# Order of two steps on TensorE in the attention loop of a four-layer graph network: the scores of two steps in a row, then the value products and denominators of two steps

## The reference

```python
q = (x @ Wq + bq).reshape(n, H, DK)          # H = 8 heads, DK = 64
k = (x @ Wk + bk).reshape(n, H, DK)
v = (x @ Wv + bv).reshape(n, H, DK)
logits = einsum('ehd,ehd->eh', q[rows] / sqrt(DK), k[cols]) + att_bias
p = exp(logits - row_max[rows])
denom = segment_sum(p, rows)
y = segment_sum((p / denom[rows])[:, :, None] * v[cols], rows)
out = y.reshape(n, 512) @ Wo + bo
```

## Time and profile before

| | |
|---|---|
| median of three runs | 1270.24 us |
| the three runs | 1258.51, 1270.24, 1271.98 us |
| span of the profiled execution | 1264.5 us |
| time of the profiled execution outside the span | none is given |
| TensorE busy | 1203.6 us (95%) |
| VectorE busy | 864.5 us (68%) |
| ScalarE busy | 431.7 us (34%) |
| stretch from the first scores of the loop to the end | 282 us, from 982.6 us on |

### The profile page before, as it was taken

The page is one execution under the profiler, slowest core; times in us unless marked ns, Lnnn a source line. Parts: engine busy times, 40 slices in busy tenths (PEclk is TensorE's granted clock), DMA queues, the critical chain, the costliest instruction groups (busy, mean ns, idle before and its releaser), DMA issues.

```text
span 1264.5 us, 22058 instructions
## 1 busy us (share of the span) xinstructions
PE 1203.6 (95%) x8483; PEld 547.2 (43%) x8484; DVE 864.5 (68%) x1180; ACT 431.7 (34%) x585; POOL 309.5 (24%) x220
## 2 busy tenths in 40 slices
PE   6989888999898999999999999999999999999997
PEld 2334333323443343344445454454332455555563
DVE  7577666434444555552478874658999799899897
ACT  1445556322232221213301003145551454444344
POOL 2001110000010243454555654555462000000000
PEclk9989999999998999999999999999999899999999
DMA  8568885798798788643122213113222666465552
GB/s 325 208 225 301 292 298 165 281 358 310 244 360 284 276 313 278 220 97 114 3 50 35 50 3 69 2 2 44 33 33 56 234 206 230 167 203 198 189 181 107
DMA packets 64414, 222.78 MB, mean 176 GB/s; under 512 B 31226, under 2 KB 36090, under 8 KB 48360
## 3 DMA queue, kind: packets, MB, share of 16 engines
q1 hardware_dynamic: 34794, 156.40, 35.6%
q0 software_dynamic: 25184, 53.10, 16.5%
q10 hardware_dynamic: 4350, 12.07, 2.8%
HBM read 198.94 MB, written 59.94 MB: 205 GB/s over the span
## 4 chain that ended last, share of the span: by engine, by line
PE 64%; DVE 11%; DMA 10%; issue 8%; SPq 5%; ACT 3%; ACTq 0%; DVEq 0%
PE PS L1812 24%; PE PS L1761 10%; PE PS L2057 4%; PE PS L1616 4%; PE PS L2044 4%; DMA R<-R 4%; DVE R L1147 4%; DVE R L1182 3%; PE PS L1634 3%; SPq L602 3%; PE PS L1686 2%; PE PS L1926 2%; SPq L600 2%; PE PS L2077 2%; PE PS L2106 2%
## 5 line engine op out<-in xcount | busy, mean ns | idle before, releaser
L787 POOL DMA_INDIRECT bias_d<-R x160 | 272.9, 1706 | 331.5 <-DMA bias_d<-R 220.2
L1812 PE MATMUL PS<-R 128*128 128x512 f16 x1300 | 298.4, 381 | 0.0
L1812 PEld LDWEIGHTS PS<-R 128*128 128x128 f16 x1300 | 120.5, 98 | 180.5 <-issue 49.8
L1572 ACT ACTIVATE R<-PS 128x1024 f32<-128x1024 f32 (+1 forms) x100 | 100.4, 1005 | 144.0 <-PE PS L2044 143.9
L1686 PE MATMUL PS<-R,XX 125*128 125x512 f16 (+2 forms) x612 | 131.0, 344 | 16.2 <-ACT R L1361 7.5
L1761 PE MATMUL PS<-W,XX 128*128 128x512 f16 x600 | 136.1, 386 | 4.7 <-DVE R L985 2.7
L1182 DVE SCALAR_TENSOR_TENSOR R<-R,W 128x1024 f32<-128x1024 f32 (+1 forms) x68 | 133.9, 1985 | 8.7 <-ACT R L1572 7.2
L1147 DVE CUSTOM_DVE_ANT_0 R<-PS,R 128x1250 f16<-128x1250 f32 x80 | 116.8, 1460 | 5.5 <-PE PS L1980 2.9
L901 DVE TENSOR_SCALAR R<-W,R 125x1250 f16<-125x1250 f16 x160 | 89.5, 606 | 42.4 <-PE PS L1686 27.6
L2044 PE MATMUL PS<-R 128*128 128x256 f16 (+3 forms) x800 | 107.4, 277 | 1.4 <-DVE R L1147 1.1
L2057 PE MATMUL PS<-R 128*32 128x256 f32 (+1 forms) x1600 | 105.7, 382 | 0.7 <-DVE R L1182 0.3
(11 more groups left out here) (226 smaller groups left out, 1395.6 us busy)
## 6 DMA issues: line engine op xcount, KB each, us to landing
bias_d<-bias_d POOLq DMA_DIRECT2D x39, 1280.0 KB, 8.5
R<-in_basis_s SPq DMA_DIRECT2D x32, 1024.0 KB, 6.6
W<-in_basis_s SPq DMA_DIRECT2D x28, 1024.0 KB, 6.3
W<-bias_d SPq DMA_DIRECT2D x27, 1024.0 KB, 4.9
R<-bias_d SPq DMA_DIRECT2D x13, 1024.0 KB, 5.0
R<-key_d SPq DMA_DIRECT2D x20, 500.0 KB, 3.8
R<-R SPq DMA_DIRECT2D x120, 80.0 KB, 5.9
W<-bias_d SPq DMA_DIRECT2D x7, 904.0 KB, 4.6
```

The source lines that it names most:

```text
L787: pool.indirect_dma_start(bias_d, bass.IndirectOffsetOnAxis(ap=idx[:, c:c + 1], axis=0), attr[:, c, :], None, bounds_check=DUMP + GC * P - ...
L1572: S.activation(ER[:, n % 4, :].rearrange("p (h r) -> p h r", h=4)[:, :, 0:w], PS[:, 2 * (n % 2):2 * (n % 2) + 2, :].rearrange("p a (e r) - ...
L1812: ins = T.matmul(mm_out(SUM_BANK(s, i), D), lhs, rhs, start=n == 0, stop=n == len(terms) - 1)
```

## The change

In the loop, the scores of step n + 2 were issued ahead of the products of step n, at every step. Now at every even n the scores of steps n + 2 and n + 3 are issued ahead, and at odd n none. The order becomes S(0) S(1) S(2) S(3) W(0) W(1) S(4) S(5) W(2) W(3) and so on; the projections keep their place behind W of steps 13 and 17 of a block, which are odd. No instruction is added or removed, and every wait stays in front of the same instruction. Nothing changes on the other engines' queues.

```diff
             for n in range(STEPS):
                 rb, m = divmod(n, QUADS * NT)
-                if n + 2 < STEPS:
+                if n % 2 == 0 and n + 2 < STEPS:
                     scores(n + 2)
+                    scores(n + 3)
                 weighted(n)
```

## The result

The changed kernel took 1260.38 us (median of 20 runs, 1254.20 to 1273.32) where the one before took 1268.56 (20 runs, 1258.51 to 1274.08). The ratio is 0.9948, with a 95% interval from 0.9926 to 0.9971: between 3.7 and 9.4 us less, most likely 6.6. It is taken over the fast runs alone, which leaves out the run of 1273.32 us; the two medians lie 8.2 us apart, inside the same interval. Forecast were 4.7 us less and no change by the 1% bound. The profiled execution has a span of 1254.1 us. That is 10.4 under the span of before, which is more than the change is worth, so the trace has to be cut by stage.

A forecast was written before the change was run, and what follows sets the result against it. TensorE was taken to set the pace, VectorE following at nine tenths. Gains of 3.9 + 1.0 + 0.8 less 1.0 for the clock gave 4.7 us off the 1270.24 median, about 1265.5; forecast 1262 to 1268 (0.65), measurement range 1256 to 1272.

The forecast's parts named there:

- 1% bound: Whole kernel: about 1%, 12.7 us, is what a measurement can tell from no change; 0.88 was put on staying within.
- (a): TensorE's changes between S and W in the loop: one each way per two steps, saving 0.23 us a pair, 4.63 us.
- (b): Waits of the reordered scores and bias loads: all covered, by over 1.5 us for E(n + 1), 3 us for biases.
- (c): Middle blocks: VectorE's extras make W(69) 1.2 us late, so a block gains 1.3 us, three blocks 3.9.
- (d): Last block: nine pairs save 1.9 us, VectorE takes 0.9 of it, a gain of 1.0.
- (e): First block: nine pairs save 2.1 us, W(0) loses its cover and costs 1.30, a gain of 0.8.
- (f): Start of the loop: TensorE's clock may rise later, costing 0 to 2.1 us, taken as 1.0.
- The sum: Whole loop: 3.9 + 1.0 + 0.8 less 1.0 for the clock, 4.7 us off.
- two signs of being wrong: A block outside 52.8 to 54.0 us, or stretches ahead of the loop differing by more than the loop does.
- VectorE keeps up: Rival in the blocks: VectorE's extras fit the pauses, all the saving stays, 8 to 10 us, 1261 us; chance 0.10.
- Gaps that stay: Rival at TensorE's hand-overs: gaps return between S and S, W and W; 1 to 3.5 us slower, about 1272; chance 0.13.
- VectorE further back: Rival in a block's first half: V(n + 2) waits for E(n + 2), some 0.3 us a pair; 1270, no change; chance 0.12.

The follow-up runs named there:

- experiment 3: Changed kernel with the old order for the first two steps, S(2) W(0) S(3) W(1), pairs from step 2 on: 1257.69 us, ratio 0.9898 to the kernel before.
- experiment 1: Changed kernel plus a one-column matmul between a pair's two S, four forms: pair 4.643, 4.755 (128 x 128; 16 bit, fp32), 4.827, 4.873 us (128 x 32), against 4.618.
- experiment 5: Kernel of experiment 3 with the reading of the denominators moved from VectorE to ScalarE: 1256.03 us, ratio 0.9906 to the kernel before.

## Why the prediction was right

*(a) Hand-overs.* Right, and shown twice: 0.24 us a pair against 0.23 forecast, and the four extra matmuls put the gap at the change of form.

*(b) The waits.* Right. In the middle blocks TensorE had no wait for ScalarE and VectorE none for a bias load. One queue wasn't seen: E(61) stood behind the reading of the sums and began at 1139.36 instead of 1137.5, when E(60) was through. L1191 held V(61) longer still, so it cost nothing of its own.

*(c) VectorE.* Right in mechanism and size. Forecast were a W(69) that is 1.2 us late and a block gain of 1.3. W(69) starts 27.45 us after S(60), and 26.28 after it with the reciprocals cut, so it is 1.17 late; the cut is worth 1.20 a block, and the gain was 1.42. The place was wider than written: late were W(65), W(67) and W(69), since the second W of a pair meets its weighing first. The "continuous 22.1 us" were 22.0.

*(d) The last block.* 1.15 against 1.0.

*(e) and (f), the start.* The account was wrong, and that the outcome was as close as 0.8 us is in part luck, since two errors worked against each other. Against S(0) the first block gained 0.6 us, where 0.8 less 1.0 was forecast. W(3) came 1.32 us later than before (16.95 against 15.63 us after S(0)), where 1.3 and 1.0 were forecast, and the eight pairs behind it gave 1.93 back. The step that failed is "It ran [...] under the wait of S(3) for the row maxima, which came back by 991.44": S(3) before started 2.71 us behind W(0), as it does in experiment 3 with 2.73, because W(0) itself took that long at half the clock. The maxima were there sooner; in the changed kernel S(3) starts 7.6 us after S(0), not 8.8. These 1.25 us come back, against the 1.32 that W(0) takes at full clock: moving it would have cost 0.1 us, by this estimate, where (e) took 1.3. The cost is the clock's: W(0) took 2.56 us and W(1), at half for its first 0.8 us, 1.81 instead of 1.43, together 1.6 where (f) took 1.0 between bounds of 0 and 2.1. Neither term looked at the load of biases ahead of V(2), which had W(2) start at 13.2 us before and limits what experiment 3 gets back to 1.7 us.

*The sum* was 4.7 of 6.0 us in the loop, within the interval of the ratio. It is short by 0.8 at the start, 0.4 in the middle blocks and 0.15 in the last. The two signs of being wrong did not come up: the block of 53.2 us lies within 52.8 to 54.0, and the stretches ahead of the loop differ by 4.3 us, less than the loop does.

*The time.* The median of 1260.38 us is not in the 1262 to 1268 that the forecast had 0.65 on; it lies in the wider range for a measurement and nearest to the 1261 of the rival in which VectorE keeps up. Of the 5.1 us between it and the 1265.5 forecast, 1.7 are the median of before, lower over twenty runs than over three. The rest is the shortfall of the sum and the spread of the runs. The time alone would have picked the wrong case; the blocks of 53.2 us, not 52.3, tell them apart.

*The rivals.* Gaps that stay: excluded by experiment 1. VectorE keeps up (8 to 10 us): not in this kernel. It is what the order gives once V(61) isn't held; with the start mended too, in experiment 5, the loop is 12.3 us shorter. VectorE further back: no; there was no wait of V for E inside the half block.

## What to carry to other kernels

Count the changes of form on TensorE as you count instructions: two kinds of matmul in turn cost about 0.1 us per change, and doing two or more of each in a row saves it if buffers and waits allow. Then read the next engine against the new pace stretch by stretch, not over the block: VectorE was 92% busy in the block and still late in its first half. Two cures were worth the same 1.2 us: 2.4 us less work in the middle, or one reading of 0.6 us, with its wait of 0.5, moved away from the start. When work is reordered, ask what the first and the last turn of the loop had hidden, and look for the next thing that holds the same place: here a load behind the row maxima.

## What the runs showed of the hardware

- A matmul of one column in the 128 x 32 form between matmuls of the 128 x 128 form cost 0.21 us, one of the same form 0.03; fp32 at full width 0.14.
- GpSimd's subtraction of 128 x 512 elements took 1.16 us beside a VectorE that was idle nearly throughout and up to 12.03 us beside VectorE's weighings. Where it stood beside them, it ended 1.0 us after the end of a weighing. Most weighings there took 1.94 to 2.16 us, as without it. Some took longer: one in each middle block of the kernel with subtractions of 8.2 us took 2.75 to 2.79 us, and one in the kernel with the divisions on GpSimd took 3.14.
- With TensorE's clock at half, the value products and denominators of a step took 2.56 us to the next ones, against 1.32 at full.
- The stretch ahead of the loop, the same work in all fourteen traces but for a small memset, ended between 973.9 and 991.6 us, while the three middle blocks of a trace repeat within 0.05 us in most of them. That the spread between runs of one kernel lies there too is likely, but only single traces of each kernel were read.
